# Reordering each engine's instructions within the slot of a software-pipelined memory-attention stage

## The reference

```
Q = layernorm(hidden) @ Wq.T          # 8 heads of 128; K, V from a memory of 256 rows
for _ in range(3):
    scores = einsum('bhsd,hnd->bhsn', xi, K) * beta
    w = entmax15(scores)              # threshold tau from the sorted scores, then square(clip(x - tau, 0))
    xi = einsum('bhsn,hnd->bhsd', w, V)
out = xi.reshape(B, S, H * hd) @ Wo.T
```

## Time and profile before

| | |
|---|---|
| median of 3 runs | 2476.78 us |
| the profiled execution | 2480.28 us |
| its span, first to last instruction | 2478.5 us |
| memory stage, first centring to last | 654.8 to 1508.9 us |
| slots of the stage between these | 47 |

### The profile page before, as it was taken

The page is one execution under the profiler, slowest core; times in us unless marked ns, Lnnn a source line. Parts: engine busy times, 40 slices in busy tenths (PEclk is TensorE's granted clock), DMA queues, the critical chain, the costliest instruction groups (busy, mean ns, idle before and its releaser), DMA issues. The chain is left out here.

```text
span 2478.5 us, 28184 instructions
## 1 busy us (share of the span) xinstructions
PE 1999.3 (81%) x8474; PEld 1430.8 (58%) x8474; DVE 1430.5 (58%) x3222; ACT 1140.1 (46%) x2757; POOL 630.9 (25%) x1932
## 2 busy tenths in 40 slices
PE   2878788898666687678669666589999999999997
PEld 1544554555554575567557555358657756865774
DVE  3566563232488898899889888333344245335324
ACT  1333232101388898888889888112312221231321
POOL 2322431010244454454444443210010010001000
PEclk9778788999877798789879877899999999999998
DMA  5000000001000000000000000000000000000000
GB/s 211 1 0 0 0 0 0 0 0 51 1 1 1 1 1 1 1 1 1 1 1 1 1 1 1 0 1 1 1 0 10 1 0 10 1 1 0 9 1 9
DMA packets 6593, 19.91 MB, mean 8 GB/s; under 512 B 958, under 2 KB 3966, under 8 KB 5183
## 3 DMA queue, kind: packets, MB, share of 16 engines
q1 hardware_dynamic: 6462, 18.30, 2.0%
HBM read 16.20 MB, written 2.10 MB: 7 GB/s over the span
## 5 line engine op out<-in xcount | busy, mean ns | idle before, releaser
L1273 ACT ACTIVATE mem_arena<-mem_arena,r_shift 128x256 f32<-128x256 f32 x864 | 384.5, 501 | 12.6 <-POOL r_shift L1212 12.4
L1044 DVE BATCH_NORM_STATS2 r_moments<-mem_arena 128x6 f32<-128x512 f32 x576 | 371.0, 684 | 2.0 <-ACT mem_arena L1273 1.7
L1359 PE MATMUL r_bank<-G,r_wT 128*128 128x256 f32 x1024 | 291.0, 447 | 32.4 <-ACT mem_arena L1273 26.8
L1359 PEld LDWEIGHTS r_bank<-G,r_wT 128*128 128x128 f32 x1024 | 227.1, 228 | 80.1 <-issue 43.2
L1815 ACT ACTIVATE e_PT<-e_banks 128x512 f32<-128x512 f32 x160 | 95.5, 597 | 312.0 <-PE e_banks L1955 311.8
L1556 DVE TENSOR_REDUCE e_NM<-e_banks 128x2 f32<-128x1024 f32 (+3 forms) x128 | 105.3, 825 | 223.1 <-PE e_banks L1930 223.1
L1373 PE MATMUL r_bank<-ident,mem_arena 128*128 128x128 f32 x576 | 107.1, 318 | 144.7 <-DVE mem_arena L1060 144.7
L1021 DVE MAX8 r_top<-r_bank 128x8 f32<-128x256 f32 x384 | 152.6, 422 | 83.0 <-PE r_bank L1359 82.3
L1373 PEld LDWEIGHTS r_bank<-ident,mem_arena 128*128 128x128 f32 x576 | 79.7, 164 | 170.7 <-DVE mem_arena L1060 160.4
L1966 PE MATMUL e_banks<-e_PT,e_V 128*128 128x256 f32 (+3 forms) x512 | 172.3, 450 | 0.0
L1359 PE MATMUL r_bank<-G,r_xnT 128*128 128x256 f32 x512 | 130.0, 413 | 27.9 <-ACT mem_arena L1273 23.6
(11 more groups left out here) (308 smaller groups left out, 3978.3 us busy)
## 6 DMA issues: line engine op xcount, KB each, us to landing
w<-in_w SPq DMA_DIRECT2D x3, 1024.0 KB, 13.6
X<-in_x SPq DMA_DIRECT2D x1, 2048.0 KB, 7.5
out_x<-X SPq DMA_DIRECT2D x4, 512.0 KB, 2.9
w_in<-in_w_in SPq DMA_DIRECT2D x1, 1156.0 KB, 8.9
mem_arena<-in_wq SPq DMA_DIRECT2D x1, 1024.0 KB, 17.3
mem_arena<-in_wo SPq DMA_DIRECT2D x1, 1024.0 KB, 19.7
gate<-in_gate SPq DMA_DIRECT2D x1, 1024.0 KB, 4.8
up<-in_up SPq DMA_DIRECT2D x1, 1024.0 KB, 7.0
```

What stands on the lines that cost most here:

```text
L1044: last = dve.bn_stats(moments[:, a.lane, 2 * p:2 * p + 2, :].rearrange("p two c -> p (two c)"), u[a.lane][:, 2 * p:2 * p + 2, :].rearrange ...
L1273: last = act.activation(u[a.lane][:, h, :], u[a.lane][:, h, :] if k else scores[:, h, :], ACT.Relu, bias=shift[:, a.lane, h:h + 1])
L1359: last = pe.matmul(scores[:, h, :], lhs, (G1 if a.first else G2)[:, h, i, :], start=i == 0, stop=i == 1)
```

## The change

Only the four lists change, and the number of slots (one fewer). Every engine runs the same instructions with the same operands and the same waits. The lists are written from another place in the cycle, so ScalarE's slot n now holds what belongs to units one further back, and TensorE's and GpSimd's one further on; that alone means nothing, as no engine waits for a slot. What moves, with VectorE's slot n as the frame (m is the unit scored in it, S0 to S3 its four score groups):

- TensorE: before, T2(m-4), S0, T3(m-4), S1, S2, S3, O2 and O3(m-5), tile transposes, T0, T1(m-3), O0, O1(m-4), where T and O are transposes and output products of a pair; after, O3(m-5), T2, T3(m-4), S0, S1, S2, S3, O0, O1, O2(m-4), tile transposes, T0, T1(m-3).
- VectorE, between the last `largest` of m and the `bound` of m: before, 3+1+1+1 moments and 5 weights; after, 2+2+1+1+1 moments and 7 weights. Between `bound` and the last `largest`: one moment and two weights fewer in total, and `out_stats` and `out_norm` now stand here.
- ScalarE: before `start`'s clips, 3 clips of pass 3 and then pass 0 heads 0 and 1; after, 4 clips of pass 3 and then pass 0 heads 0, 1 and 2; `columns` of pairs 2 and 3 of m-4 come before, between and after the last clips of pass 0.
- GpSimd: `out_rstd` moves from the middle of the chain that begins with `centre` to behind `start`; `second_moment` of pass 0 comes before the `newton` of pass 3.

```diff
--- before.py
+++ after.py
@@ -898,7 +898,7 @@
 
 DVE_HEADS = (0, 1, 2, 3, 4, 5, 6)
 ACT_HEADS = (7,)
-FIRST_SLOT, LAST_SLOT = -2, TILES * STEPS - 1 + 6
+FIRST_SLOT, LAST_SLOT = -2, TILES * STEPS - 1 + 5
 
 NPAIR = NHM // 2
 PASSES = 4
@@ -1075,38 +1075,37 @@
                 dve.tensor_tensor(X[:, a.tile, :], X[:, a.tile, :], onorm[:], ALU.add).then_inc(x_ready, 1)
 
             for n in range(FIRST_SLOT, LAST_SLOT + 1):
-                tile_rows(Unit(n + 1))
+                weights(Unit(n - 4), 3)
+                take_moments(Unit(n - 3), 2, 2, 3)
+                weights(Unit(n - 4), 4)
+                take_moments(Unit(n - 2), 1, 0)
+                invert(Unit(n - 3), 2)
                 take_moments(Unit(n - 2), 1, 1)
-                invert(Unit(n - 3), 2)
                 clear(Unit(n - 1))
-                weights(Unit(n - 4), 4, 5, 6)
+                weights(Unit(n - 4), 5, 6)
+                take_moments(Unit(n - 2), 1, 2)
                 bound(Unit(n - 1))
-                take_moments(Unit(n - 2), 1, 2, 3)
-                tile_stats(Unit(n + 2))
+                out_stats(Unit(n - 5))
+                take_moments(Unit(n - 2), 1, 3)
                 take_moments(Unit(n - 3), 3, 0)
                 take_moments(Unit(n - 1), 0, 0)
-                take_moments(Unit(n - 3), 3, 1, 2)
-                largest(Unit(n - 0), 0)
+                out_norm(Unit(n - 5))
+                take_moments(Unit(n - 3), 3, 1)
                 invert(Unit(n - 2), 1)
                 take_moments(Unit(n - 1), 0, 1)
+                largest(Unit(n - 0), 0, 1)
+                take_moments(Unit(n - 3), 3, 2)
+                take_moments(Unit(n - 1), 0, 2)
+                tile_stats(Unit(n + 2))
+                tile_rows(Unit(n + 1))
                 take_moments(Unit(n - 3), 3, 3)
-                largest(Unit(n - 0), 1)
-                take_moments(Unit(n - 1), 0, 2)
-                largest(Unit(n - 0), 2)
+                take_moments(Unit(n - 1), 0, 3)
+                largest(Unit(n - 0), 2, 3)
                 invert(Unit(n - 3), 3)
-                take_moments(Unit(n - 1), 0, 3)
-                largest(Unit(n - 0), 3, 4, 5)
-                weights(Unit(n - 3), 0)
                 invert(Unit(n - 1), 0)
-                weights(Unit(n - 3), 1)
-                largest(Unit(n - 0), 6, 7)
-                weights(Unit(n - 3), 2)
-                take_moments(Unit(n - 2), 2, 0, 1, 2)
-                out_stats(Unit(n - 5))
-                weights(Unit(n - 3), 3)
-                take_moments(Unit(n - 2), 2, 3)
-                out_norm(Unit(n - 5))
-                take_moments(Unit(n - 1), 1, 0)
+                largest(Unit(n - 0), 4, 5, 6, 7)
+                take_moments(Unit(n - 2), 2, 0, 1)
+                weights(Unit(n - 3), 0, 1, 2)
 
         @block.gpsimd
         def _(pool):
@@ -1220,27 +1219,27 @@
                 pool.tensor_tensor(ors[:], ove[:], T["half_neg"][:, 0:1], ALU.pow).then_inc(ors_ready, 1)
 
             for n in range(FIRST_SLOT, LAST_SLOT + 1):
-                second_moment(Unit(n - 2), 0)
-                tile_rstd(Unit(n + 1))
-                newton(Unit(n - 2), 0)
-                centre(Unit(n - 1))
-                square(Unit(n - 1))
-                running_sum(Unit(n - 1), 0)
-                running_sum(Unit(n - 1), 1)
-                running_sum(Unit(n - 1), 2)
-                mean_and_gap(Unit(n - 1))
-                out_rstd(Unit(n - 6))
-                mean_square(Unit(n - 1))
-                add_gap(Unit(n - 1))
-                second_moment(Unit(n - 3), 2)
-                add_room(Unit(n - 1))
-                newton(Unit(n - 3), 2)
-                step_back(Unit(n - 1))
-                start(Unit(n - 1))
-                second_moment(Unit(n - 2), 1)
-                newton(Unit(n - 2), 1)
-                second_moment(Unit(n - 3), 3)
-                newton(Unit(n - 3), 3)
+                newton(Unit(n - 1), 0)
+                centre(Unit(n - 0))
+                square(Unit(n - 0))
+                running_sum(Unit(n - 0), 0)
+                running_sum(Unit(n - 0), 1)
+                running_sum(Unit(n - 0), 2)
+                mean_and_gap(Unit(n - 0))
+                mean_square(Unit(n - 0))
+                add_gap(Unit(n - 0))
+                second_moment(Unit(n - 2), 2)
+                add_room(Unit(n - 0))
+                newton(Unit(n - 2), 2)
+                step_back(Unit(n - 0))
+                start(Unit(n - 0))
+                tile_rstd(Unit(n + 2))
+                out_rstd(Unit(n - 4))
+                second_moment(Unit(n - 1), 1)
+                newton(Unit(n - 1), 1)
+                second_moment(Unit(n - 2), 3)
+                second_moment(Unit(n - 0), 0)
+                newton(Unit(n - 2), 3)
 
         @block.scalar
         def _(act):
@@ -1299,37 +1298,34 @@
                     act.activation(wT[:, a.lane, 2 * p:2 * p + 2, :, :], bank[:, TB + p % 2, :], ACT.Square).then_inc(wT_ready, 1)
 
             for n in range(FIRST_SLOT, LAST_SLOT + 1):
-                columns(Unit(n - 4), 2)
-                clip(Unit(n - 1), 0, 6, 7)
-                columns(Unit(n - 4), 3)
-                newton_root(Unit(n - 3), 3)
-                clip(Unit(n - 2), 2, 0, 1, 2, 3, 4)
-                newton_root(Unit(n - 1), 0)
-                clip(Unit(n - 2), 2, 5)
-                weights(Unit(n - 3), 7)
-                clip(Unit(n - 1), 1, 0)
-                clip(Unit(n - 2), 2, 6)
-                clip(Unit(n - 1), 1, 1)
-                clip(Unit(n - 2), 2, 7)
-                clip(Unit(n - 1), 1, 2, 3)
-                tile_columns(Unit(n + 1))
-                clip(Unit(n - 1), 1, 4)
-                columns(Unit(n - 3), 0)
-                clip(Unit(n - 1), 1, 5)
-                columns(Unit(n - 3), 1)
-                newton_root(Unit(n - 2), 2)
-                clip(Unit(n - 1), 1, 6)
-                bound_root(Unit(n - 0))
-                clip(Unit(n - 1), 1, 7)
-                clip(Unit(n - 2), 3, 0, 1, 2)
-                clip(Unit(n - 0), 0, 0, 1)
-                clip(Unit(n - 2), 3, 3, 4, 5)
-                clip(Unit(n - 0), 0, 2)
-                clip(Unit(n - 2), 3, 6)
-                clip(Unit(n - 0), 0, 3)
-                clip(Unit(n - 2), 3, 7)
-                clip(Unit(n - 0), 0, 4, 5)
-                newton_root(Unit(n - 1), 1)
+                clip(Unit(n - 3), 1, 5)
+                tile_columns(Unit(n - 1))
+                clip(Unit(n - 3), 1, 6, 7)
+                columns(Unit(n - 5), 0)
+                newton_root(Unit(n - 4), 2)
+                columns(Unit(n - 5), 1)
+                bound_root(Unit(n - 2))
+                clip(Unit(n - 4), 3, 0, 1, 2, 3)
+                clip(Unit(n - 2), 0, 0, 1, 2)
+                clip(Unit(n - 4), 3, 4)
+                clip(Unit(n - 2), 0, 3)
+                clip(Unit(n - 4), 3, 5)
+                clip(Unit(n - 2), 0, 4)
+                clip(Unit(n - 4), 3, 6)
+                clip(Unit(n - 2), 0, 5)
+                newton_root(Unit(n - 3), 1)
+                columns(Unit(n - 5), 2)
+                clip(Unit(n - 4), 3, 7)
+                clip(Unit(n - 2), 0, 6, 7)
+                columns(Unit(n - 5), 3)
+                clip(Unit(n - 3), 2, 0, 1, 2, 3)
+                newton_root(Unit(n - 4), 3)
+                clip(Unit(n - 3), 2, 4)
+                newton_root(Unit(n - 2), 0)
+                clip(Unit(n - 3), 2, 5, 6, 7)
+                clip(Unit(n - 2), 1, 0)
+                weights(Unit(n - 4), 7)
+                clip(Unit(n - 2), 1, 1, 2, 3, 4)
 
         @block.tensor
         def _(pe):
@@ -1389,14 +1385,12 @@
                         last.then_inc(out_done, 1)
 
             for n in range(FIRST_SLOT, LAST_SLOT + 1):
-                transpose(Unit(n - 4), 2)
-                score(Unit(n - 0), 0)
-                transpose(Unit(n - 4), 3)
-                score(Unit(n - 0), 1, 2, 3)
-                output(Unit(n - 5), 2, 3)
-                tile_transpose(Unit(n + 1))
-                transpose(Unit(n - 3), 0, 1)
-                output(Unit(n - 4), 0, 1)
+                output(Unit(n - 4), 3)
+                transpose(Unit(n - 3), 2, 3)
+                score(Unit(n + 1), 0, 1, 2, 3)
+                output(Unit(n - 3), 0, 1, 2)
+                tile_transpose(Unit(n + 2))
+                transpose(Unit(n - 2), 0, 1)
 
 
 def experts_block(nc, T, out):
```

## The result

The kernel after takes 2489.86 us (five runs, 2487.65 to 2496.34), the kernel before 2475.42 beside it (five runs, 2474.46 to 2477.82): ratio 1.0059, interval 1.0043 to 1.0074. It is slower by about 14 us, 0.6%, where 42 us less were predicted. The profiled execution has a span of 2488.1 us, 9.6 more than before.

What follows compares the result with a forecast made beforehand. A loop around one slot (`largest`, `bound`, S0, scores) sets the pace; mid slots 8.2 + 8.05 + 1.0 = 17.3 us, output four 68.7, cycle 207.1 against 218.7, 42.5 us less over 44 slots: 2434 us, range 2407 to 2474.

Steps and rivals of the forecast that it cites:

- The clock term: TensorE, mid slots: T2 and T3 ahead of S0 bring the clock up sooner; low-clock penalty falls from 2.0 to 1.0 us.
- the 0.5 us for T3 out of the run: TensorE, S0 to the next `largest`: T3 leaves the run of scores, which becomes 0.5 us shorter.
- The first rival: TensorE, mid slots: the clock rises no sooner, penalty stays 2.0, mid slot 18.25, 12 slots 214.7, 2462 us; chance 0.19.
- The cover in output slots: TensorE behind S3: O0 to O2, under 3 us, then T0 and T1, needed by `columns` only 3.3 us or more after `largest`.
- The chain: From `largest` over `bound` to S0: VectorE's part grows by 0.5 us to 6.9; S0 begins at 8.2, against 7.7.
- The step of seven weights: VectorE, between `largest` and `bound`: seven weights take 2.0 us, from three in 0.87, 0.29 each.
- ScalarE's fourth clip: ScalarE, ahead of pass 0: the fourth pass-3 clip has no slack left and costs nothing; 0.1 late allowed.
- The rival "slower": Mid slots: clock low through S0 and half of S1, penalty 2.8, slot 19.05, 12 slots 221.1, 2486 us; chance 0.14.
- A new wait: At ScalarE's fourth clip or S3: something late by 1 us in each slot, gain gone, 2477 us; chance 0.10.
- The drain: End of the stage: one slot fewer, without work on the last unit's path; nothing, within 5 us either way.

Runs made afterwards that it cites:

- e11: Kernel after with e4's unused matmuls and e7's output order, plus one moment moved behind `bound` and three pass-3 clips before two of pass 0: 2422.08 us, 0.9771.
- e10: Kernel after with e5's small unused matmul and e7's output order together: 2431.90 us, 0.9809 to the kernel before.
- e4: Kernel after with 12 unused matmuls in each mid slot: six behind S3, five before T2, one before S0: 2427.05 us, 0.9785 to the kernel before.
- e5: Kernel after with one unused matmul of 128 columns between T3 and S0, in mid slots alone: 2445.02 us, 0.9862 to the kernel before.
- e2: Kernel before with the new TensorE list alone: 2549.91 us, 1.0283 to the kernel before.
- e3: Kernel after with VectorE's old list, entries of new and finished tiles staying at their new places: 2481.24 us, 1.0007 to the kernel before.
- e1: Kernel after with T3 put back between S0 and S1: 2504.45 us, 1.0100 to the kernel before.
- e7: Kernel after with TensorE's order behind S3 changed to tile transposes, O0, O1, T0, T1, O2: 2476.69 us, 0.9992 to the kernel before.
- e9: Kernel after with VectorE's pass-2 moments of pairs 2 and 3 before four of the five weights, behind GpSimd's running sums: 2481.31 us, 1.0007.

## Why the prediction was wrong

The reading of what bounds the kernel held: the loop of `largest`, chain, S0 and the run of scores is the slot in every mid slot looked at here, in e11 too. Three terms of the sum were wrong. A cycle took 223.2 us instead of 207.1: of the 16.1, the clock made 8.6 and the chain 2.1 in the eight mid slots, and the output four made 5.4. (This is bookkeeping; the clock's part depends on the others, as said below.) With the first and the last mended (e10) a cycle takes 208.2 us and the kernel 2431.9, where the prediction had 207.1 and 2434.

**The clock term was the largest.** The prediction let the penalty of the low clock in a mid slot fall from 2.0 to 1.0, since T2 and T3 run right ahead of S0 "with a break of 0.4". The break is 0.56, and the penalty did not fall: a mid slot of the cycle is (223.2 - 74.1) / 8 = 18.64 us, less 8.46 and 8.05 leaves 2.1; against e4, whose clock stays at its upper level, the scores of units 19 to 23 lose 2.4. That transposes bring on the clock was right (e5); that they do so across that break was wrong. The same TensorE list with a break of 0.27 (e2) has mid slots of 17.16 us, with 0.12 (e5) of 17.23, with 0.56 (after) of 18.89. The break isn't the whole of it: e3 has one of 0.64 and mid slots of 18.24, some with S0 at 3.45. Nor is the penalty a term that can be added to the others, as the sum had it. The chain of e2 is 0.7 us shorter than that of e5, and their mid slots are equally long, 17.38, 17.22, 17.14, 17.11, 17.09 in units 18 to 22 against 17.62, 17.34, 17.21, 17.14, 17.10: what the chain gave, the low clock took. In e1 it was the other way about, and the slots stayed at 18.2 and 19.3. And the 0.5 us for T3 out of the run was not there in mid slots, because with T3 inside the run the clock had risen 0.8 us sooner behind the start of S0 (e1): work moved from inside the low spell to a place ahead of it, with a pause behind it, saved nothing. The step counted a gain of 0.5 in work and one of 1.0 in clock, and mid slots got neither.

The first rival had this result for mid slots, with its reason, "the break of 0.4 us may break the run". 214.7 us for its cycle, 3.1 more in mid slots (2.1 of chain, 1.0 of clock) and 5.4 in output slots are the 223.2. The Trainium skill ("TensorE: Matmul & The Clock Gate", Part 4: PE-mode transpose), by whose rule transpose-mode work does not count for the clock in the same way, gives the same rival for another reason. The traces disagree with that reason: in e5, with transposes and one small matmul right ahead of the scores, the clock rises 1.8 to 2.4 us behind the start of that matmul, where without that matmul it rises 2.8 to 6.2 us behind the start of the scores.

**The cover in output slots was counted wrong.** The prediction named O0 to O2 as "12 of 16 matmuls, under 3 us" in front of T0 and T1. The text ahead of the prediction counts scores by rows of the trace (32, for 16 matmuls) and outputs by matmuls (16, which are 32 rows), and the step compared the two as like with like. Each of these matmuls has two rows; a pair of either kind has four matmuls, 8 rows, and takes 1.8 us. The three pairs are 24 rows and 5.34 us. Moreover the tile transposes stand behind them, and the prediction named only T0's `columns` as waiting, not `tile_columns`, which stands ahead of `bound_root` on ScalarE. The four slots took 74.1 instead of 68.7, a part of it by the clock that fell behind the longer break; with the order mended, and no fall of the clock, 69.4 (e7).

**The chain grew by 0.8, not 0.5.** The step of seven weights at 0.29 each took its duration from a stretch where GpSimd was not at its running sums. Beside them a weight takes longer (0.41 in the mean of that row), and that makes the 0.26 by which `bound` and S0 are late against the prediction. The moments took what was predicted, and GpSimd was in time. e9 gives 0.17 of it back, and what remains is open. ScalarE's fourth clip cost nothing in the kernel after, where pass 0 begins 0.32 us behind `bound` as before, and 0.4 once `bound` came earlier (e3).

**The range and the other rivals.** The rival "slower" gave 2486 us, near the result, from a penalty of 2.8 in each mid slot. It is 1.7 in one half of them and 2.8 in the other, 2.3 in the mean, below the 2.5 from which the rival was to decide: the size is right by chance. "A new wait" was right in kind (ScalarE at `tile_columns`), at a place that it did not name and at under half of its size: 5.4 us a cycle, 20 in all, where 1 us in each slot would be 44. The prediction weighed these cases as alternatives, and three of them came together; its range had no room for the sum. The drain, costed at nothing within 5, gave 6.8 back.

The mid slots alternate between S1 at 1.95 and 3.07 us because the clock rises 3.7 and 5.9 us behind the start of S0 in turn. What makes it do so in a steady loop is open, and with it how long a mid slot with a low spell will be before it is run.

## What to carry to other kernels

Where TensorE pauses in each round of a loop, read the granted clock before counting its work: moving work out of a run at the low clock gains nothing, unless it closes the pause in front of the run; a single small unused matmul in the right place was worth 45 us here, the same one elsewhere nothing. And do not carry a low spell as a fixed price into a sum: a chain shorter by 0.7 us bought nothing in e2 against e5. Count the rows of a group in the trace before naming it as cover, and follow each thing behind it on the engine that waits, not only the first. Take an instruction's duration from a stretch in which the other engines do what they will be doing beside it.

## What the runs showed of the hardware

- Transposes on TensorE helped to bring on the higher clock when scores followed with next to no pause: in e5 (pause 0.12 us) it rose 1.1 to 1.6 us behind the start of S0 in units 20 to 24, in e2 (0.27 us) 3.0 in unit 22, and with 0.56 us (after) 3.7 or 5.9.
- The length of mid slots with a low spell settled at 17.1 us for chains of 7.7 (e2) and 8.46 us (e5) alike.
- Work added to TensorE shortened the kernel, 2489.9 to 2427.1 us with twelve unused matmuls a mid slot.
- VectorE's fp32 clip with per-row operands (128 x 256) takes longer while GpSimd works on 128 x 128 fp32 sums: four in 1.65 us there, against two in 0.61 later in the same slot (the row at 1008.52) and three in 0.87 before. The rows show them side by side and not why; in e9 five weights, all but the first two behind the sums, still took 1.79.
